# A transformer block stack on one core: the threshold of the second attention split between VectorE and GpSimd, and the epsilon of both norms moved

## What is computed

```python
def _layernorm(x, axis=-1, eps=1e-05):
    m = jnp.mean(x, axis=axis, keepdims=True)
    v = jnp.var(x, axis=axis, keepdims=True)
    return (x - m) / jnp.sqrt(v + eps)

def sparsemax_lastdim(z):
    z_sorted = jnp.flip(jnp.sort(z, axis=-1), axis=-1)
    cs = jnp.cumsum(z_sorted, axis=-1)
    rho = jnp.arange(1, d + 1, dtype=z.dtype)
    support = 1.0 + rho * z_sorted > cs
    k = jnp.maximum(jnp.sum(support, axis=-1, keepdims=True), 1)
    cs_k = jnp.take_along_axis(cs, k - 1, axis=-1)
    tau = (cs_k - 1.0) / k.astype(z.dtype)
    return jnp.maximum(z - tau, 0.0)

x = x + attn_a(_layernorm(x))      # softmax, 16 heads
x = x + ffn(_layernorm(x))
x = x + attn_b(_layernorm(x))      # causal sparsemax, 16 heads
x = x + ffn(_layernorm(x))
```

## Time and profile before

| | |
|---|---|
| median of three runs | 600.16 us (597.83 to 601.16) |
| the profiled execution | 598.14 us, span 596.4 us |
| PE (TensorE matmul) busy | 568.1 us, 95% |
| DVE (VectorE) busy | 495.8 us, 83% |
| ACT (ScalarE) busy | 415.0 us, 70% |
| POOL (GpSimd) busy | 385.3 us, 65% |
| TensorE clock granted | 0.997 of full speed |

### The profile page before, as it was taken

The page is one execution under the profiler, slowest core; times in us unless marked ns, Lnnn a source line. Parts: engine busy times, 40 slices in busy tenths (PEclk is TensorE's granted clock), DMA queues, the critical chain, the costliest instruction groups (busy, mean ns, idle before and its releaser), DMA issues.

```text
span 596.4 us, 19146 instructions
## 1 busy us (share of the span) xinstructions
PE 568.1 (95%) x6702; PEld 438.2 (73%) x6702; DVE 495.8 (83%) x1445; ACT 415.0 (70%) x1038; POOL 385.3 (65%) x817
## 2 busy tenths in 40 slices
PE   8778999999999999999999998999999999999895
PEld 6555666777777777777677786788888888888774
DVE  3679889898988898987788888788888899889763
ACT  1104678778887777788888767767887777777652
POOL 4755556667776667677667776666666677764422
PEclk9989999999999999999999999999999999999999
DMA  7656666566766666745545644335544445441000
GB/s 220 178 157 146 164 155 152 131 151 156 175 152 154 150 150 150 176 117 140 134 117 126 156 128 103 90 90 128 118 119 120 130 128 129 115 121 36 12 20 23
DMA packets 74657, 76.25 MB, mean 128 GB/s; under 512 B 10348, under 2 KB 68908, under 8 KB 70092
## 3 DMA queue, kind: packets, MB, share of 16 engines
q1 hardware_dynamic: 63636, 68.09, 45.0%
q10 hardware_dynamic: 10920, 6.88, 5.5%
HBM read 46.86 MB, written 23.33 MB: 118 GB/s over the span
## 4 chain that ended last, share of the span: by engine, by line
PE 70%; DVE 19%; issue 4%; ACT 3%; POOL 3%; DMA 1%; SPq 0%; ACTq 0%; DVEq 0%; POOLq 0%
PE banks L1630 15%; PE banks L1571 10%; PE banks L1606 9%; PE banks L1472 7%; PE banks L1535 7%; DVE top L1156 5%; DVE top L1155 3%; PE banks L1524 3%; DVE neg_shift L1150 2%; PE banks L1525 2%; PE banks L1504 2%; PE banks L1574 2%; DVE top_sums L1177 1%; DVE top_sums L1180 1%; PE banks L1482 1%
## 5 line engine op out<-in xcount | busy, mean ns | idle before, releaser
L1366 ACT ACTIVATE probs_t<-banks 128x512 f32<-128x512 f32 (+1 forms) x496 | 259.2, 551 | 72.3 <-PE banks L1606 47.8
L1150 DVE TENSOR_REDUCE neg_shift<-banks 128x2 f32<-128x512 f32 x256 | 165.7, 681 | 31.5 <-PE banks L1571 30.0
L1630 PE MATMUL banks<-probs_t,v_ext 128*32 128x256 f32 (+1 forms) x2048 | 116.8, 357 | 0.0
L1571 PE MATMUL banks<-k_stack,q_stack 72*128 72x256 bf16 x512 | 99.7, 276 | 8.0 <-DVE neg_shift L1150 3.3
L1156 DVE MAX8 top<-banks 128x8 f32<-128x256 f32 x256 | 106.1, 414 | 0.0
L1606 PE MATMUL banks<-q_stack,k_stack 75*128 75x256 bf16 x512 | 98.4, 273 | 0.3 <-ACT probs_t L1366 0.2
L1155 DVE MAX8 top<-banks 128x8 f32<-128x128 f32 x256 | 74.1, 290 | 19.8 <-PE banks L1580 19.4
L1026 POOL TENSOR_TENSOR hidden<-up_tanh,gate_half 128x256 f32<-128x256 f32 x93 | 68.3, 736 | 28.6 <-DVE up_tanh L1209 23.5
L1630 PEld LDWEIGHTS banks<-probs_t,v_ext 128*32 128x32 f32 x2048 | 55.4, 109 | 38.8 <-issue 12.8
L1571 PEld LDWEIGHTS banks<-k_stack,q_stack 72*128 72x128 bf16 x512 | 40.4, 98 | 48.1 <-DVE neg_shift L1150 36.4
L1524 PE MATMUL banks<-f_xT_high,w_gate_up 128*128 128x256 f32 x192 | 57.5, 322 | 2.3 <-DVE up_tanh L1209 2.0
(11 more groups left out here) (123 smaller groups left out, 1366.9 us busy)
## 6 DMA issues: line engine op xcount, KB each, us to landing
q_stack<-q_image SPq DMA_DIRECT2D x93, 192.0 KB
k_stack<-k_image SPq DMA_DIRECT2D x93, 192.0 KB
q_image<-qk_parts SPq DMA_DIRECT2D x32, 192.0 KB, 2.4
k_image<-qk_parts SPq DMA_DIRECT2D x32, 192.0 KB, 2.1
q_image<-qk_parts SPq DMA_DIRECT2D x32, 128.0 KB, 2.9
o_image<-out_t SPq DMA_DIRECT2D x32, 128.0 KB, 1.8
out_compact<-o_image SPq DMA_DIRECT2D x32, 64.0 KB
rdenominators<-r_image SPq DMA_DIRECT2D x16, 128.0 KB, 3.5
```

The costliest lines, as they stand in the source:

```text
L1150: dve.tensor_reduce(m.nm[:, n % STACKS, h, :], scores.rearrange("p (q k) -> p q k", q=TT), AX.X, ALU.max, negate=True).then_inc(reduced, 1)
L1366: act.activation(m.pt[:, (n * Q + g) % GROUPS, i, 0:size], shifted_bank(n, j)[:, 0:size], ACT.Exp if is_soft(n) else ACT.Relu, scale=SCALE ...
L1571: ins = pe.matmul(scores[:, qt * T:(qt + 1) * T], qs[0:STACK, h, qt * P:(qt + 1) * P], ks[0:STACK, h, :], start=True, stop=True)
L1630: ins = pe.matmul(out_bank[32 * i:32 * i + 32, at + skip:at + T], v_windows(v, kt)[:, Q * g + i, :], m.pt[:, (n * Q + g) % GROUPS, i, kt * ...
```

## The change

The middle one of the three operations of the threshold goes from VectorE to GpSimd, where it becomes two (minus one; times 1/k), at step 17 (S1). The maximum stays on VectorE and moves from step 16 to step 19 (S3), where it waits for GpSimd. The transposition of the shift and its copy go from step 22 to 24 (S6 to S8), its load from 23 to 25 (S7 to S9), and the semaphore counts four instead of three steps. Both norms' epsilon is added by GpSimd between minus the mean and the power.

```diff
-          tau=16, shift_split_soft=17, shift_split_plain=18, excess=20, shift=23, load_shift=24,
+          tau=16, tau_scale=17, tau_max=19, shift_split_soft=17, shift_split_plain=18, excess=20, shift=23, load_shift=24,
...
-PLAIN = dict(a_bn=-30, a_norm=-25, v=-16, take_v=-14, store_k=-13, load_q=-13, shift_split_plain=20, shift=22,
-             load_shift=23, load_rden=61, xb=67, f_aggr=72, up1=85, hid1=89, down=92)
+PLAIN = dict(a_bn=-30, a_norm=-25, v=-16, take_v=-14, store_k=-13, load_q=-13, shift_split_plain=20, shift=24,
+             load_shift=25, load_rden=61, xb=67, f_aggr=72, up1=85, hid1=89, down=92)
...
             def rstd_a(n):
                 pool.wait_ge(a_var, n * TT + TT)
                 pool.tensor_scalar(m.a_neg[:, :], m.a_mv[:, :, 0], -1.0, None, ALU.mult).then_inc(a_rstd, 1)
+                pool.tensor_scalar(m.a_ve[:, :], m.a_mv[:, :, 1], EPS, None, ALU.add).then_inc(a_eps, 1)
                 pool.wait_ge(a_eps, n + 1)
...
+            def scale_sums(n):
+                b = n - B
+                cs = m.cs[:, :, :, :].rearrange("p h q k -> p (h q k)")
+                pool.wait_ge(tau_step, b * 4 + 1)
+                pool.tensor_scalar(cs, cs, -1.0, None, ALU.add).then_inc(tau_step, 1)
+                pool.wait_ge(tau_step, b * 4 + 2)
+                pool.tensor_tensor(cs, cs, m.cc[:, CC["invk"]:CC["invk"] + 256], ALU.mult).then_inc(tau_step, 1)
...
                 if (n := due(step, "shift_split_soft")) is not None and is_soft(n):
                     split_shift(n)
+                if (n := due(step, "tau_scale")) is not None and not is_soft(n):
+                    scale_sums(n)
...
                     dve.bn_aggr(m.a_mv[:, tt, :], m.a_stats[:, tt, :]).then_inc(a_var, 1)
-                dve.wait_ge(a_var, n * TT + TT)
-                dve.tensor_scalar(m.a_ve[:, :], m.a_mv[:, :, 1], EPS, None, ALU.add).then_inc(a_eps, 1)
...
                 dve.tensor_tensor_scan(cs, m.cc[:, CC["seg"]:CC["seg"] + 256], z, 0.0, ALU.mult,
                                        ALU.add).then_inc(tau_step, 1)
-                dve.wait_ge(tau_step, b * 3 + 1)
-                dve.scalar_tensor_tensor(cs, cs, -1.0, m.cc[:, CC["invk"]:CC["invk"] + 256], ALU.add,
-                                         ALU.mult).then_inc(tau_step, 1)
-                dve.wait_ge(tau_step, b * 3 + 2)
+
+            def tau_max(n):
+                b = n - B
+                c = m.cs[:, :, :, :].rearrange("p h q k -> p (h q) k")
+                dve.wait_ge(tau_step, b * 4 + 3)
                 dve.tensor_reduce(m.nm[:, n % STACKS, :, :].rearrange("p h q -> p (h q)"), c, AX.X, ALU.max,
                                   negate=True).then_inc(tau_step, 1)
...
                 if (n := due(step, "tau")) is not None and not is_soft(n):
                     tau(n)
+                if (n := due(step, "tau_max")) is not None and not is_soft(n):
+                    tau_max(n)
```

More of the change, by code:

```diff
@@ L956, in rstd_f @@
                 pool.tensor_scalar(m.f_neg[:, :], m.f_mv[:, :, 0], -1.0, None, ALU.mult).then_inc(f_rstd, 1)
+                pool.tensor_scalar(m.f_ve[:, :], m.f_mv[:, :, 1], EPS, None, ALU.add).then_inc(f_eps, 1)
                 pool.wait_ge(f_eps, n + 1)
@@ L985, in split_shift @@
                 else:
-                    pool.wait_ge(tau_step, (n - B) * 3 + 3)
+                    pool.wait_ge(tau_step, (n - B) * 4 + 4)
                 if n > 0:
@@ L1112, in aggregate_f @@
                     dve.bn_aggr(m.f_mv[:, tt, :], m.f_stats[:, tt, :]).then_inc(f_var, 1)
-                dve.wait_ge(f_var, n * TT + TT)
-                dve.tensor_scalar(m.f_ve[:, :], m.f_mv[:, :, 1], EPS, None, ALU.add).then_inc(f_eps, 1)
             def rope_cos(n, which, use):
@@ L1174, in tau @@
                 cs = m.cs[:, :, :, :].rearrange("p h q k -> p (h q k)")
-                c = m.cs[:, :, :, :].rearrange("p h q k -> p (h q) k")
                 dve.wait_ge(reduced, (n + 1) * H)
```

## The result

The changed kernel takes 602.63 us in the median of its runs (598.59 to 608.3), the kernel before on the same chips 597.72 us (595.49 to 602.53): a ratio of 1.0064, with a 95% interval of 1.004 to 1.0089. Ratios leave out an execution over 1.5% above the fastest of its kernel, here the one of 608.3 us, so they are not the quotients of the medians. The predicted time was 601.6 us, which is 1.0024 of the 600.16 us it started from; the predicted ratio lies under the interval, so the size was short although the absolute time was near. With the bound of 0.5% that the prediction used, 1.0064 is slower, but the interval starts at 1.004, within "no change".

A forecast was written before the change was run, and what follows sets the result against it. TensorE was taken as the first limit, so VectorE's relief returns only TensorE's waits for it. Terms: +2.1 (plain), +0.45 (items 16 to 20), -1.4 (soft and start), +0.3 (tail) = +1.4 us on 600.16: 601.6 us, range 596.5 to 606.

The forecast's parts named there:

- within 0.5%: Whole run: time within 3 us of 600.16 us, about what a measurement can tell from no change; chance 0.49.
- items 16 to 20: First plain items: VectorE or ScalarE's norm late behind GpSimd's longer list, then some returned; together +0.45 us, from -1.0 to +2.5.
- the tail: End of the kernel: ScalarE already waited 0.55 us for GpSimd's bias at 577.23, so the longer chain costs +0.3 us, whole.
- the start: Five or so items of the start, where TensorE waits more for VectorE: -0.1 us each, -0.5 us.
- The steady plain item: Items 20 to 28: later bias and norm delay probabilities for TensorE's second pass of S10; +0.23 us each, +2.1 us.
- The soft items: Soft part: VectorE without the epsilon shortens TensorE's wait; -0.1 us each for nine items, -0.9 us.
- the term for item 17: Item 17: the maximum on VectorE waits for GpSimd's pair, and everything queued behind it comes later; +0.55 us.
- items 18 to 20: Item 18: -0.3 us from the epsilon that goes; items 19 and 20, VectorE late after the scan: 0.2 us each come back.
- The rule on the shared port: GpSimd and VectorE share a buffer read port, so the pair would slow VectorE; forecast unchanged, as VectorE reads scores from other memory.
- The relief: Rival: earlier heads at S1 to S3 remove TensorE's wait at S6, 4.4 us come back; 594.4 us, chance 0.18.
- The shift's load: Rival: the load lands too late behind loads of keys, each plain item waits at S14; 609 us, chance 0.05.
- The rival on GpSimd's chain: Rival: chain to ScalarE's norm 0.4 us longer than reckoned, 13 plain items cost 0.63 each; about 606.8 us, chance 0.20.

The follow-up runs named there:

- eighth kernel: The changed kernel with the first of GpSimd's two threshold operations as a subtraction of a tile of ones; one execution, 602.65 us.
- fifth kernel: The changed kernel with the threshold's middle operation back on VectorE behind the scan and the shift's transposition and copy one step sooner; ratio to the kernel before 0.9993.
- the seventh: The changed kernel with the softmax's product on GpSimd one step later, behind the threshold's pair; ratio to the kernel before 1.0077.
- the sixth: Changed kernel, middle operation back on VectorE, shift's copy one step sooner, GpSimd's epsilon only in the soft items' attention norm; ratio to the kernel before 0.998.
- the ninth kernel: Kernel before with soft items' attention epsilon on GpSimd; items 16 to 20 with maximum at S3, middle operation on VectorE, copy moved; 593.96 us against 598.28, ratio 0.9935.
- the first: The kernel before with both norms' epsilon on GpSimd and nothing else; 598.84 us against 598.52, ratio 0.9992.
- the tenth: The kernel before with the epsilon on GpSimd in the soft items' attention norm alone; 600 us against 598.28, ratio 1.002.

## Why the prediction was right, and where it was off

**The total: near in the time, short in the change.** The forecast change was +1.4 us; the profiles differ by 2.9 us and the medians by 4.9. That 601.6 us came within 1.0 us of the median measured is in part luck: the 600.16 us it was added to were 2.4 us above the 597.72 us of the 20 executions, and this error and the short sum, 3.5 us, point opposite ways. The likeliest of the three outcomes in the chances was "within 0.5%", and the ratio measured, 1.0064, lies just outside it. What was short in the sum, against the profiles, are items 16 to 20 (0.7 us), the tail (0.5) and the start (0.3), below.

**The steady plain item: right, in size and in mechanism.** Forecast +0.23 us, measured +0.23 in the mean and 0.24 in most (16.18 us), and each link as written: idle time on VectorE behind the scan 0.89 us (about 0.8), no wait of the maximum for GpSimd, the bias begun at 408.15 (407.95, in a frame that is 0.07 us later), the norm at 408.38 (408.2), the second pass at 410.33 (410.16), with its wait for the probabilities. The copy's part in it was shown by moving it, the chain's by the halves of the change. One thing was luck: the pair on GpSimd takes 1.69 us from start to end and not the 1.15 I reckoned, and it did not matter, because the cut of the shift waits for the maximum.

**The soft items: right.** -0.1 us each and nine of them, shown with the epsilon alone; VectorE gained 0.36 us there, and TensorE took under a third of it. The start's -0.5 us did not show (-0.2 at item 5), but no profile here can tell it: the granted clock fell for some us in the start of both kernels, in other places.

**Items 16 to 20: mis-sized, +0.45 forecast and +1.13 measured.** The terms were +0.6 and +0.55 for items 16 and 17; both cost 1.4. I had the pair on GpSimd at 1.15 us, since its first operation was priced by the cast, 0.40 us; it takes 0.86, outside both bounds. VectorE's wait at item 17 was 1.16 us where I had 0.55. Beyond the size, the term for item 17 named the wrong link: with VectorE's wait cut to 0.48 us nothing came back, because ScalarE's norm is late by the same GpSimd list. The returns at items 18 to 20 were larger too, -1.72 us where I had -0.7. At item 18 it was -0.37 us against -0.3 forecast, and it goes with the epsilon, as forecast: the epsilon alone has -0.48 us there (behind +0.23 at item 17), the threshold alone -0.13. The 1.35 us at items 19 and 20, where I had 0.4, come with the maximum's move; with the threshold alone they are 2.31 us, with the epsilon alone under 0.1.

**The tail: mis-sized, +0.3 forecast and +0.8 measured.** The norm I charged, with its 0.55 us of wait, moved by nothing of its own. The one before it moved by 0.55 us (568.82 - 559.58 = 9.24 us behind the last scan, 8.69 before), of which 0.2 come back by the end. The other +0.48 lies in item 30, which I had at nothing; the threshold alone makes 0.20 us there and the epsilon alone 0.15, and what makes the rest is open.

**The rule on the shared port.** The Trainium skill (Perfetto Trace Analysis, Optimizing Scalar/DVE Operations) warned that work moved between GpSimd and VectorE may not help. The outcome agrees, but the mechanism shown here is another: VectorE reads its first head 1.67 us behind the scan with the middle operation or without it, and on GpSimd's list the pair takes 1.7 us. Contention does show in the durations, 0.65 us for the operation beside GpSimd against 0.424 alone.

**The rivals.** The relief did not reach TensorE (its wait rose from 4.4 to 7.2 us). The shift's load was no wait in the steady items, though issued at 409.91. The 3.5 us of landing time that spoke against this rival did not hold everywhere: near the end of the changed kernel the weight load that needed the shift went 5.6 us after the issue (543.09 and 537.51), with a wait of 0.40 us, and in the eighth kernel 6.4 us after it. The rival on GpSimd's chain was true in kind at items 16 and 17 and false in the other items: its 0.2 us of room was not used up there.

## What to carry to other kernels

Before an operation is moved off a busy engine, look at what stands beside it: behind this scan VectorE waits for scores anyway, so for the first head the operation was free there (1.67 us with it and without it), and the maximum was worth moving only in the five items in which it was not. Follow the receiving engine's list through to the engine that waits for its end (here ScalarE's norm, then the probabilities), and look for a small operation there, such as the copy, that will now fall in between. A place in a list that serves all items may want another value in the items where two stages meet; here that choice was the only gain that the intervals show.

## What the runs showed of the hardware

A one-input operation (add a constant) on GpSimd over 128 x 256 float32 values took 0.86 us in all 16 items, a two-input one in the same place 0.72 in the median (0.74 at most), the cast to bfloat16, which has one input too, 0.40. So the number of inputs does not give the price here. The same epsilon of two columns is 0.22 us there and 0.17 on VectorE in the median.

```profile
L1005 POOL TENSOR_SCALAR top_sums<-top_sums x16: 860/862/863, 312.2 to 560.3; 128x256 f32<-128x256 f32 x16
```

Between the products of items 3 and 4, where these kernels hardly differ, the runs took from 14.3 to 20.8 us. TensorE had idle time there for which the profile gives no releaser ("issue"), 0.69 us in the fifth kernel and 3.01 us in the seventh, and what is behind it was not tried. It is not the whole difference: after the longer idle time the granted clock fell. In the seventh kernel it was 0.50 of full speed from 55 to 60 us, the lower of TensorE's two levels, and the same pair of matmuls took 0.63 us instead of 0.38. In the fifth kernel it stayed at 1.00. First a row of the fifth, then two of the seventh:

```profile
50.72 0.38 PE L1581 MATMUL banks<-k_stack,q_stack 72*128 72x256 bf16 x2 [0.69 <-issue]
```
```profile
53.22 0.38 PE L1581 MATMUL banks<-k_stack,q_stack 72*128 72x256 bf16 x2 [3.01 <-issue]
...
55.19 0.63 PE L1581 MATMUL banks<-k_stack,q_stack 72*128 72x256 bf16 x2
```

The fifth, the sixth and the ninth kernel, which had no such fall in this stretch, took 14.3, 15.1 and 14.6 us for it, the kernel before, where the clock fell ahead of it (0.50 from 38 to 41 us), 14.9, and the first, with 0.50 from 54 to 60 us, 19.1. The ninth and the tenth run the same lists up to here and took 14.6 and 17.1 us, so the offset is not the edit's. Two single profiles of such kernels can therefore differ by over 1% before the first changed plain item, and are compared from a point behind it, and medians of few executions only beside their granted clocks.
